# Router logits with the turned tokens as the stationary operand and the 16 gate columns moving

## The reference

```
scores = sigmoid(xf @ gate_w.T)            # xf: 2048 x 512, gate_w: 16 x 512
scores = scores + expert_bias
group_scores = scores in 4 groups of 4, best of each; keep the 2 best groups
idx = top 4 of the kept scores;  w = scores without bias at idx, normalised to sum 1
y = sum over the 4 picks of w * expert(xf);  z = shared expert (2 x 352 hidden)
out = layernorm(x + y + z)
```

## Time and profile before

| | |
|---|---|
| median of three runs | 2260.56 us |
| the profiled execution's own time | 2261.06 us |
| its span, first to last instruction | 2259.2 us |
| granted TensorE clock, mean over the span | 0.975 |
| PE busy | 2135.0 us, 95% |
| DVE, ACT, POOL busy | 1444.7, 1187.5, 1372.4 us |
| gate stage, first turn to the start of the shared expert | 1424.1 to 1457.3 us of the span |
| shared expert's start to the counts | 1457.3 to 1489.4 |
| counts to the first scatter | 1489.4 to 1499.0 |
| scatters, to the start of the experts' stage | 1499.0 to 1607.3 |

### The profile page before, as it was taken

How to read it: one execution, slowest core, us unless ns; L and a number is a source line. 1 busy time by engine, 2 the same in 40 slices (tenths; PEclk the granted TensorE clock), 3 DMA queues, 4 the chain that set the end, 5 groups by cost and what they waited for, 6 DMA issues and landing times. The chain is left out here.

```text
span 2259.2 us, 43212 instructions
## 1 busy us (share of the span) xinstructions
PE 2135.0 (95%) x13185; PEld 1952.6 (86%) x13186; DVE 1444.7 (64%) x4586; ACT 1187.5 (53%) x3946; POOL 1372.4 (61%) x1952
## 2 busy tenths in 40 slices
PE   5899999999999999999999999896599999989997
PEld 3799999999999999999999998475499999979875
DVE  5688888888888888888888888543122222222277
ACT  2567767766767766766766767520133333323222
POOL 2787667767767767767767766046722203787484
PEclk8999999999999999999999999898699999999998
DMA  5600540000000000000000000334533323666365
GB/s 151 210 22 20 170 135 20 4 22 23 1 22 22 12 12 22 15 8 22 15 8 22 2 1 1 123 114 159 172 127 119 119 79 122 196 189 193 118 186 162
DMA packets 88026, 177.50 MB, mean 79 GB/s; under 512 B 11616, under 2 KB 40992, under 8 KB 87712
## 3 DMA queue, kind: packets, MB, share of 16 engines
q1 hardware_dynamic: 54224, 100.92, 14.4%
q10 hardware_dynamic: 23328, 40.73, 5.4%
q0 software_dynamic: 10288, 33.58, 4.6%
HBM read 108.06 MB, written 67.13 MB: 78 GB/s over the span
## 5 line engine op out<-in xcount | busy, mean ns | idle before, releaser
L957 PE MATMUL bank<-whi,xT_lo 128*128 128x384 f32 x1024 | 367.3, 359 | 4.2 <-PEq L180 3.2
L959 PE MATMUL bank<-whi,xT_hi 128*128 128x384 f32 x1024 | 345.6, 338 | 0.0
L958 PE MATMUL bank<-wlo,xT_hi 128*128 128x384 f32 x1024 | 345.5, 337 | 0.0
L810 POOL TENSOR_TENSOR cross<-nat,rope_tables 128x128 f32<-128x128 f32 x256 | 111.4, 435 | 363.9 <-DVE nat L659 363.9
L736 ACT COPY probT<-bank 128x128 f32<-128x128 f32 (+3 forms) x256 | 109.2, 426 | 303.6 <-PE bank L571 303.4
L1788 DVE TENSOR_TENSOR shlo<-bank,shhi 128x256 fp32r<-128x256 f32 x76 | 32.3, 425 | 287.7 <-ACT shhi L1713 287.7
L957 PE MATMUL bank<-ring_hi,xslo 128*128 128x352 f32 x600 | 203.2, 339 | 10.4 <-issue 9.0
L672 DVE SCALAR_TENSOR_TENSOR prob<-taken,prob 128x32 f32<-128x32 f32 (+15 forms) x256 | 207.0, 808 | 0.9 <-ACT prob L747 0.8
L957 PEld LDWEIGHTS bank<-whi,xT_lo 128*128 128x128 f32 x1024 | 193.8, 189 | 4.8 <-issue 3.5
L959 PE MATMUL bank<-ring_hi,xshi 128*128 128x352 f32 x600 | 195.3, 326 | 0.0
L958 PE MATMUL bank<-ring_lo,xshi 128*128 128x352 f32 x600 | 194.9, 325 | 0.0
(11 more groups left out here) (273 smaller groups left out, 6374.9 us busy)
## 6 DMA issues: line engine op xcount, KB each, us to landing
staged<-in_wexp SPq DMA_DIRECT2D x80, 544.0 KB, 4.0
slots_in<-zeros SPq DMA_DIRECT2D x41, 512.0 KB, 6.6
xslot<-slots_in ACTq DMA_DIRECT2D x76, 256.0 KB, 2.7
slots_out<-yslot ACTq DMA_DIRECT2D x76, 256.0 KB, 2.0
wraw<-in_wh SPq DMA_DIRECT2D x16, 768.0 KB, 4.3
slots_out<-zeros SPq DMA_DIRECT2D x9, 512.0 KB, 6.5
acc<-in_x SPq DMA_DIRECT2D x4, 1024.0 KB, 12.3
wo<-in_Wo SPq DMA_DIRECT2D x16, 256.0 KB, 2.6
```

Of the source, the lines that this page charges most:

```text
L810: pool.tensor_tensor(cross[:, :, :], nat[:, a.two, :, 0:2 * ROT], sin, ALU.mult).then_inc(s_mult, 1)
L957: pe.matmul(out, wl_, xh_, start=first, stop=False)
L958: pe.matmul(out, wh_, xl_, start=False, stop=False)
L959: return pe.matmul(out, wh_, xh_, start=False, stop=last)
```

## The change

The operands of the gate product change places. The turned tokens of a tile (128 x 128) are loaded into the array, and the 16 gate columns move; the result is 128 tokens by 16 logits and goes straight to its place in the logits' bank. A step therefore has four products of 16 columns instead of one of 512 columns. The 16 steps of all four chunks add into one bank: the first product alone starts it, the last alone closes it. The copy to `logitT`, the turning back, their buffer and three semaphores go; ACT's sigmoid waits for the last gate product instead of the last turn back; `up(0, 0)` no longer waits for the last copy.

```diff
                 def gate_logits(i):
                     c, k = divmod(i, KC)
-                    if k == 0:
-                        wait_for(pe, s_lgc, c - 1)
                     pe.wait_ge(s_raw, i + 1)
-                    pe.matmul(bank[2 + c % 2][0:E, :], gateT[:, k, :], raw[:, i % RAWS, :],
-                              start=(k == 0), stop=(k == KC - 1)).then_inc(s_gl, 1)
-
-                def logits_back(c):
-                    pe.wait_ge(s_lgc, c + 1)
                     for j in range(TPC):
                         n = c * TPC + j
-                        mm = pe.transpose(b_logits[:, n * E:(n + 1) * E], logitT[:, j * P:(j + 1) * P], ident[0:E, 0:E])
-                    mm.then_inc(s_gb, 1)
+                        mm = pe.matmul(b_logits[:, n * E:(n + 1) * E], raw[:, i % RAWS, j * P:(j + 1) * P], gateT[:, k, :],
+                                       start=(i + j == 0), stop=(i + j == NCH * KC + TPC - 2))
+                    mm.then_inc(s_gl, 1)
...
-                    if m:
-                        pe.wait_ge(s_silu, m)
-                    else:
-                        pe.wait_ge(s_lgc, NCH)
+                    wait_for(pe, s_silu, m)
...
                     gate_logits(i)
-                    if i % KC == 2 and i > KC:
-                        logits_back(i // KC - 1)
                 for k in range(KC):
                     turn(0, k)
-                logits_back(NCH - 1)
...
-                act.wait_ge(s_gb, NCH)
+                act.wait_ge(s_gl, NCH * KC)
...
                 for c in range(NCH):
-                    dve.wait_ge(s_gl, (c + 1) * KC)
-                    wait_for(dve, s_gb, c)
-                    dve.tensor_copy(logitT[:, :], bank[2 + c % 2][0:E, :]).then_inc(s_lgc, 1)
                     if c + 1 < NCH:
                         piece_low(2 * c)
                         piece_low(2 * c + 1)
```

More of the change, by code:

```diff
@@ L989, in front @@
         choice, cmp, slotf = (work[:, j * NT * E:(j + 1) * NT * E].rearrange("p (n e) -> p n e", e=E) for j in range(3))
-        logitT = work[0:E, 0:CH]
         byt = work[:, 0:MAXT * E // 2].bitcast(BF16).rearrange("p (t e) -> p t e", e=E)
@@ L1009, in front @@
         by16 = pickedb
-        g_in, w_in, s_turned, s_raw, s_gl, s_lgc, s_gb, s_sig, s_r, s_pick, s_count, s_slots = (sem(n, st) for n in (
-            "gate_weights_in", "gate_tables_in", "x1_turned", "x1_raw", "gate_logits", "logits_copied", "logits_back", "sig_done", "router_step",
+        g_in, w_in, s_turned, s_raw, s_gl, s_sig, s_r, s_pick, s_count, s_slots = (sem(n, st) for n in (
+            "gate_weights_in", "gate_tables_in", "x1_turned", "x1_raw", "gate_logits", "sig_done", "router_step",
             "picked_done", "counts_done", "slots_done"))
```

## The result

| | before | after |
|---|---|---|
| median of the runs taken side by side | 2260.86 us (2258.79 to 2263.27, 6 runs) | 2274.57 us (2272.6 to 2276.61, 6 runs) |
| the profiled execution's own time | 2261.06 us | 2273.5 us |
| granted clock, mean over the span | 0.975 | 0.969 |

The account below looks back on a forecast made before the run. PE's chain through the gate loop and shared expert to the counts was taken as the bound. Shared expert 18.9 us later plus 0.8 us for earning the clock gave +19.7 us, forecast 2280 us, range 2266 to 2288.

Parts of the forecast that it names:

- The clock: Gate stage: loads with 16 columns each would not lift the clock at 1431; 0.50 until the shared expert streams.
- first rival: Gate loop: clock rises at about 1431 as before, so no change, 2259.9 us; chance 0.11.
- The loads follow the clock: Gate products: 128-column float32 loads slow with the clock, 0.111 us at 1.00 to 0.22 us at 0.50.
- second rival: Gate loop: clock stays low but loads take 0.111 us at either level, +5.5 us, 2266 us; chance 0.03.
- The passage to the end: Behind the counts: PE's delay passes through DVE and POOL in full; DVE's 14.39 us wait stays.
- The price of a step at 0.50: Gate loop: 1.04 us from turn to product plus 1.90 us for eight loads, 2.94 us a step.
- the sum's +19.7: PE's arrival at the counts: shared expert 18.9 us later plus 0.8 us for earning the clock.
- the joint of 0.12: Gate step at 0.50: about 0.12 us between the products and the next turn, added to 1.78 us of loads.
- Earning the clock in the shared expert: Shared expert's dense start at 0.50: a loss of 2.5 us instead of 1.7, 0.8 us more.
- The exchange at equal clock: Gate step at 1.00: eight loads, 0.89 us, replace the old product, about 0.86 us; worth nothing.
- third rival: Gate loop: loads hide behind each other, at most 0.08 us each, and the clock rises; 2256 us, chance 0.02.
- The scatters: POOL's 64 scatters ahead of the experts' stage: they follow the counts' delay and are themselves unchanged.

Follow-up runs that it names:

- the control: Changed kernel with 16 gate columns plus only the one bfloat16 product of 512 zero columns opening the logits' bank: 2269.28 us, ratio 1.0047.
- the padding: Changed kernel with 112 zero columns behind the 16 gate columns, 128 moving, and one product of zeros opening the logits' bank: 2255.65 us, ratio 0.9986.
- the run without the gap: Changed kernel with filling products before the gate stage to bring the clock up, and ACT's first weight rounding three steps later: 2263.11 us, ratio 1.0012.
- the two with the old product: The kernel before, 2260.86 us, and the same with filling products that bring the clock up before the gate stage, 2256.89 us, ratio 0.9986.
- 64 columns: Changed kernel with 48 zero columns behind the 16 gate columns, 64 moving, and one product opening the logits' bank: 2255.47 us, ratio 0.9989.

## Why the prediction was right

**The clock.** Right in what happened, 0.50 until 1472.37 without the rise at 1431, but the rows under it did not carry it. I took from the earlier trace rows that the level fell behind loads with single columns and not behind a stretch that streamed. That fall also came behind 1.39 us in which PE sat idle, so the gap may explain it as well. And the same kernel lost the level while it streamed 512 columns, behind the wait of 1.54 us; this row stands ahead of the one at 0.50 from 1458.70 in the earlier trace rows:

```profile
1457.27:1458.65 1.38, 1.38 (x6) 1.15 (x7) 1.38 (x2) 1.35 (x3) 0.00 (x0) 1.00 0.00 0
```

Moreover the rows show a level that was lost, and the forecast needed one that is not earned. A chance of 0.84 was more than these rows bear, and there is some luck in it. The reason is shown by the experiments. Not earned: the changed kernel stays at 0.50 through its gate stage, and the control does so from its fall to the end of the loop. Held by columns: the padding has the same loads, order and opening product as the control and takes 2255.65 instead of 2269.28 us. That 16 columns never hold the level is not shown; in the run without the gap they did for thirteen steps. How many columns it takes is open between 16 and 128. The first rival's condition, a rise near 1431, did not come; where the padding brings one, the time is still below that rival's 2259.9, since its step was priced too high.

**The loads follow the clock.** Right. 0.195 to 0.204 us at 0.50; at 1.00 twelve in 1.28 us, 0.107 (eight of the products in 1441.37 - 1440.55 = 0.82, 0.10). The second rival, 0.111 at either level, is out. The Trainium skill, "TensorE: Matmul & The Clock Gate", section "LDWEIGHTS (loading the stationary operand)", puts a load at its columns over 1.2 GHz and names no level, which is 107 ns for 128 columns: this agrees at 1.00 and is about half of what was measured at 0.50.

**The passage to the end.** Right: PE's delay reaches POOL in full (11.97, 11.96 us), and DVE's wait stays at 14.4.

**The price of a step at 0.50.** This is the term that was mis-sized, and most of the 7.3 us by which the sum's +19.7 stood above the 12.4 of the two profiled executions. I put 1.04 us for the turn, "unchanged", and 1.90 for the products, 2.94. It is 0.89 and 1.56, 2.45: thirteen steps at 0.49 make 6.4 us. The 1.04 was not the turn's loads alone; in the kernel before PEld paused 0.33 us behind them until the old product's load ("issue" means that the trace shows nothing it waited for):

```profile
1429.59 0.72 PEld L1097 LDWEIGHTS bank<-ident,acc 128*128 128x128 f32 x4 [1.69 <-issue]
1430.64 0.13 PEld L1105 LDWEIGHTS bank<-raw,gateT 128*16 128x16 f32 x2 [0.33 <-issue]
```

In the changed kernel PEld has no such pause and the next group's loads follow at once (1428.87, 1429.76 above): the turn takes 0.15 us less, the joint of 0.12 does not come, and the eight loads are 0.195 us apart, not 0.22. The rest of 1476.2 - 1469.44 = 6.8 us is the first product, 0.25 us early, and the last 24, 4.98 us instead of 5.3; the turns and the hand-over behind them took 5.05 instead of 4.9.

**Earning the clock in the shared expert.** I added 0.8 us; it cost 0.2 less than before (0.50 for 2.93 us from 1469.44, where it had been 3.41). The products there stream densely from the first on.

**The exchange at equal clock.** I called it worth nothing, 0.89 for 0.86. Wrong: a step is 1.28 against 1.55. The rows at 1.00 above have 0.82 for the new products and 0.96 for the old one to the next turn, and 0.46 against 0.59 for the turn, behind which PEld paused in the old form. It did not enter the forecast, but it hid that the third rival had a point: the step of the new form is the cheaper one once the clock is granted. What it saves there is 0.27 us a step and the three turnings back; the loads take 0.10 us each, where that rival had 0.08.

**The scatters.** I left them unchanged; they take 109.85 us, 1.5 more. In every run with the exchange it is 109.5 to 110.4, in the two with the old product 108.3 and 108.6. The wait for the first chunk's transfers has over half of it, 4.33 us where the kernel before has this row:

```profile
1513.85 0.97 POOL L1277 DMA_INDIRECT slots_in<-acc,slots  x1 [3.45 <-DMA slots_in<-acc,slots]
```

Why those transfers land later was not tried, and stays open. So does the 1.3 us that came back in the experts' stage; both are smaller than the spread between runs of one kernel.

## What to carry to other kernels

Before operands change places, ask which clock the stretch will get and not only how many array cycles it needs: a form whose step is cheaper at equal clock lost here because weight loads with few columns behind them did not earn the full clock, and held it for some steps at most, and PE's busy share, 100% in both, did not show it. Look at PEld beside PE. If the loads have to stay, columns of zeros can be nearly free, since the load sets the pace and not the columns: 128 for 16 cost 0.05 us a step at 1.00 and, with the one product that opens the bank, gave 1.1 us back.

## What was not expected of the hardware

- The full clock fell while PE was busy without a gap: 3.70 of 3.70 us and then 2.90 of 2.90 us in the control, where the step went from 1.28 to 2.45 us. The Trainium skill, "TensorE: Matmul & The Clock Gate", section "Why this matters for your kernels", advises against idle gaps between bursts of products; here their absence was not enough.
- A float32 load of 128 columns with 16 to stream behind it is followed by the next after 0.10 us at 1.00 (eight in 0.82 us) and 0.195 us at 0.50 (eight in 1.56 us). Streaming 128 columns as well changes the step only from 1.28 to 1.33 us.
- One identical loop (64 columns) ran at 0.50 and then at 1.00 within one execution, and runs of that kernel spread over 18 us, those of the changed kernel over 4. That the place of the rise differs from run to run would explain the spread; only one run was seen.
